# Four-layer graph network on one core: attention outputs kept in SBUF in place of the selections they used, selections rebuilt for the last pass, one copy moved from ScalarE to VectorE

## What is computed

```python
h = jnp.maximum(_layernorm(x, axis=-1), 0.0)
x = x + _L0_gnn_ref(h, ...)   # graph convolution with self loops, PReLU
x = x + _L1_gnn_ref(h, ...)   # segment_sum(edge_weight * h[src], dst) @ W.T + b
x = x + _L2_gnn_ref(h, ...)   # attention with 4 heads over edges and self loops,
                              # then batch norm over all 50,000 nodes, relu(out + h)
x = x + _L3_gnn_ref(h, ...)   # edge network on (h[src], h[dst]), segment_sum, node network
```

## Time and profile before

| | us |
|---|---|
| median of 3 runs | 2927.1 |
| lowest, highest of the runs | 2925.19, 2933.04 |
| the profiled execution's own time | 2935.71 |
| its span, first to last instruction | 2934.2 |

### The profile page before, as it was taken

The page is one execution under the profiler, slowest core; times in us unless marked ns, Lnnn a source line. Parts: engine busy times, 40 slices in busy tenths (PEclk is TensorE's granted clock), DMA queues, the critical chain, the costliest instruction groups (busy, mean ns, idle before and its releaser), DMA issues. The chain is left out here.

```text
span 2934.2 us, 52033 instructions
## 1 busy us (share of the span) xinstructions
PE 2190.3 (75%) x11215; PEld 1489.9 (51%) x11215; DVE 1814.1 (62%) x8347; ACT 1823.1 (62%) x4630; POOL 1440.1 (49%) x1442
## 2 busy tenths in 40 slices
PE   3376666666664777758885899666663999999996
PEld 1154444444443666648885444333332566666663
DVE  8787676766764666648886555466664544445552
ACT  0097777777774888859994333599995344444442
POOL 5177777777774666537771000000001366666663
PEclk9888888888886999988997999798997999999998
DMA  1155555555453555546662665499998111222210
GB/s 41 35 177 159 171 159 162 168 155 175 153 160 96 150 160 158 155 133 181 198 199 61 179 169 163 132 320 311 315 311 245 46 49 55 57 59 59 60 53 24
DMA packets 488297, 426.56 MB, mean 145 GB/s; under 512 B 54823, under 2 KB 384702, under 8 KB 488138
## 3 DMA queue, kind: packets, MB, share of 16 engines
q1 hardware_dynamic: 423946, 350.44, 39.7%
q0 software_dynamic: 64192, 74.09, 9.9%
HBM read 234.05 MB, written 194.13 MB: 146 GB/s over the span
## 5 line engine op out<-in xcount | busy, mean ns | idle before, releaser
L1982 POOL DMA_INDIRECT x_bx<-t_X,k_bslot x2 | 2.0, 1016 | 670.4 <-DMA t_X<-x_ve 670.1
L2235 POOL DMA_INDIRECT out_dram<-mlp_ou,mlp_iro x200 | 200.0, 1000 | 186.4 <-issue 185.8
L461 POOL DMA_INDIRECT second_xs<-t_X,second_irs x200 | 212.5, 1063 | 133.4 <-ACT second_m L1151 56.4
L461 POOL DMA_INDIRECT first_rd<-t_R,a_irs x200 | 203.4, 1017 | 119.0 <-issue 60.3
L2228 POOL DMA_INDIRECT mlp_xs<-t_X,mlp_irs x200 | 202.2, 1011 | 78.3 <-issue 59.7
L461 POOL DMA_INDIRECT a_xd<-in_x_dram,a_ird x200 | 207.9, 1040 | 65.7 <-issue 60.3
L461 POOL DMA_INDIRECT a_xs<-in_x_dram,a_irs x200 | 203.7, 1018 | 60.8 <-issue 60.5
L461 POOL DMA_INDIRECT project_xs<-t_X,project_irs x200 | 200.7, 1004 | 65.7 <-issue 62.2
L2278 DVE TENSOR_TENSOR mlp_v<-mlp_ps_r,mlp_b 126x512 f32<-126x512 f32 x50 | 34.6, 692 | 278.9 <-ACT mlp_y L2336 275.6
L2379 PE MATMUL mlp_ps_e<-mlp_h,mlp_we 128*128 128x504 f32 x400 | 188.4, 595 | 1.2 <-ACT mlp_h L2358 1.2
L2139 PE MATMUL x_ps_o<-x_ht,x_wd 128*128 128x512 f32 (+1 forms) x198 | 128.9, 738 | 80.7 <-ACT x_ht L2090 80.7
(11 more groups left out here) (391 smaller groups left out, 7036.4 us busy)
## 6 DMA issues: line engine op xcount, KB each, us to landing
t_X<-first_x SPq DMA_DIRECT2D x194, 256.0 KB, 3.1
first_x<-in_x_dram SPq DMA_DIRECT2D x97, 256.0 KB
project_x<-t_X SPq DMA_DIRECT2D x97, 256.0 KB, 3.1
x_x<-t_X SPq DMA_DIRECT2D x97, 256.0 KB, 6.3
t_X<-x_x SPq DMA_DIRECT2D x97, 256.0 KB, 6.0
out_dram<-x_ou SPq DMA_DIRECT2D x97, 256.0 KB, 6.7
t_G<-second_g SPq DMA_DIRECT2D x50, 267.8 KB
t_X<-first_xo SPq DMA_DIRECT2D x50, 252.0 KB
```

The lines of the kernel that those rows point to most:

```text
L461: pool.indirect_dma_start(dst[:, q, :], None, table, bass.IndirectOffsetOnAxis(ap=idx[:, q:q + 1], axis=0)).then_inc(s_rows, 16)
L2235: pool.indirect_dma_start(out, bass.IndirectOffsetOnAxis(ap=iro[s][:, q:q + 1], axis=0), OU[s][:, q, :], None, bounds_check=N - 1, oob_is_ ...
```

## The change

Three edits.

1. `kp.S0` becomes `[RW, NGE, GT * 128]`: 2048 bytes per group and partition, of which the four selections of a group take the first 2016. `kp.select(g, q)` is tile q's selection, `kp.rows(g)` the whole piece seen as four rows of 128. Attend writes its outputs to `kp.rows(g)`, where the group's selections stood; the squares go to `OQ`; `norms` becomes two products of 128 columns into two PSUM banks. The store to `T["O2"]` and its load are gone, and x3 finishes the slot rows in `kp.rows` and stores from there.
2. Since the selections are overwritten, mlp loads the rows of targets again (`dr`, 50 broadcast loads) and makes the selections again, four comparisons for each group, one group ahead. PE waits for `s_sel` beside `s_z`.
3. In second, the copy of `psA` to `AT` goes from the end of ACT's `body` to the end of DVE's.

```diff
@@ Keep
-        self.S0 = sb("S0", [RW, NT, RW])
+        self.S0 = sb("S0", [RW, NGE, GT * 128])
+    def select(self, g, q):
+        o = slice(q * RW, (q + 1) * RW)
+        if known(g):
+            return self.S0[:, g, o]
+        return self.S0[:, bass.ds(g, 1), o].rearrange("p a e -> p (a e)")
+    def rows(self, g):
+        if known(g):
+            return self.S0[:, g, :].rearrange("p (q d) -> p q d", q=GT)
+        return self.S0[:, bass.ds(g, 1), :].rearrange("p a (q d) -> p (a q) d", q=GT)
@@ second, vector, end of body
+            g3, r3 = t - 3, (u - 3) % 2
+            if there(g3, NGE):
+                dve.wait_ge(s_a, g3 + 1)
+                if not before(g3, 2):
+                    dve.wait_ge(s_y, g3 - 1)
+                dve.tensor_copy(AT[r3][:, :, :], psA[r3][:, 0:W4].rearrange("p (q e) -> p q e", q=GT)).then_inc(s_at, 1)
@@ second, scalar, end of body
-            r3 = (u - 3) % 2
-            if there(g3, NGE):
-                act.wait_ge(s_a, g3 + 1)
-                if not before(g3, 2):
-                    act.wait_ge(s_y, g3 - 1)
-                act.activation(AT[r3][:, :, :], psA[r3][:, 0:W4].rearrange("p (q e) -> p q e", q=GT), ACT.Copy).then_inc(s_at, 1)
@@ attend
-            g, s = t - 2, (u - 2) % 4
-            if there(g, NGE):
-                gate(kp, sp, s_o, g + 1)
-                sp.dma_start(slot_rows(T["O2"], g), OS[s][:, :, 0, :]).then_inc(s_os[s], 16)
...
-                if not before(g, 4):
-                    dve.wait_ge(s_os[s], landed(g - 4, s, 4))
-                    dve.wait_ge(s_n, g - 3)
...
-                    ins = dve.tensor_tensor(OS[s][:, 2 * b:2 * b + 2, 0, :].rearrange("p q (h c) -> p q h c", h=H),
+                    ins = dve.tensor_tensor(kp.rows(g)[:, 2 * b:2 * b + 2, :].rearrange("p q (h c) -> p q h c", h=H),
...
-                act.activation(OS[s][:, :, 1, :], OS[s][:, :, 0, :], ACT.Square).then_inc(s_sq, 1)
+                if not before(g, 4):
+                    act.wait_ge(s_n, g - 3)
+                act.activation(OQ[s][:, :, :], kp.rows(g), ACT.Square).then_inc(s_sq, 1)
...
-                ins = pe.matmul(psN[0:1, 0:256], kp.lastc[:, k:k + 1], OS[s][:, q, :, :].rearrange("p w d -> p (w d)"),
-                                start=k == 0, stop=k == NT - 1)
+                pe.matmul(psN[0:1, 0:128], kp.lastc[:, k:k + 1], kp.rows(g)[:, q, :], start=k == 0, stop=k == NT - 1)
+                ins = pe.matmul(psN[0:1, 512:640], kp.lastc[:, k:k + 1], OQ[s][:, q, :], start=k == 0, stop=k == NT - 1)
@@ x3
-                if not before(t, 4):
-                    gate(kp, sp, e_s3[u], landed(t - 4, u, 4))
-                sp.dma_start(Ve[u][:, :, :], erow2("O2", t)).then_inc(e_o[u], 16)
...
-                sp.dma_start(erows("X3", ge), Ve[se][:, :, :]).then_inc(e_s3[se], 16)
+                sp.dma_start(erows("X3", ge), kp.rows(ge)).then_inc(e_s3[se], 16)
...
-                dve.wait_ge(e_o[u], landed(t, u, 4))
-                dve.tensor_tensor(Ve[u][:, :, :], Ve[u][:, :, :], Sb[0:RW, :, :], ALU.mult).then_inc(e_v0, 1)
+                dve.tensor_tensor(kp.rows(t), kp.rows(t), Sb[0:RW, :, :], ALU.mult).then_inc(e_v0, 1)
@@ mlp, sync
+                r = u % 2
+                if not before(t, 2):
+                    sp.wait_ge(s_sel, t - 1)
+                sp.dma_start(dr[r][:, :].rearrange("p (k j) -> p k j", k=GT),
+                             T["dr"][bass.ds(t * GT, GT), :].partition_broadcast(RW)).then_inc(s_dr[r], 16)
@@ mlp, vector; called as select(0, 0) before the loop and select(t + 1, ...) at the end of body(t)
+        def select(t, v):
+            if there(t, NGE):
+                r = v % 2
+                dve.wait_ge(s_dr[r], landed(t, r, 2))
+                for q in range(GT):
+                    k = bass.ds(t * GT + q, 1)
+                    ins = dve.tensor_scalar(kp.select(t, q), dr[r][:, q * RW:(q + 1) * RW], kp.dcol[:, k], None, ALU.is_equal)
+                ins.then_inc(s_sel, 1)
@@ mlp, tensor
                 pe.wait_ge(s_z, t + 1)
+                pe.wait_ge(s_sel, t + 1)
```

More of the change, by code:

```diff
@@ L971, in sums @@
             gate(kp, pe, e_ci, t * GT + q + 1)
-            k = bass.ds(t * GT + q, 1)
-            s0 = kp.S0[:, k, :].rearrange("p a e -> p (a e)")
+            s0 = kp.select(t, q)
             pe.matmul(psC[0:RW, 128 * q:128 * (q + 1)], s0, M[r][:, q, :], start=True, stop=True).then_inc(e_co, 1)
@@ L1225, in sums @@
             pe.wait_ge(s_ci, g * GT + q + 1)
-            s0 = kp.S0[:, g * GT + q, :]
+            s0 = kp.select(g, q)
             pe.matmul(psC[0:RW, 128 * q:128 * (q + 1)], s0, M[s][:, q, :], start=True, stop=True).then_inc(s_co, 1)
@@ L1538, in body @@
                     k = g5 * GT + q
-                    ins = pe.matmul(psS[0:RW, q * SW:(q + 1) * SW], kp.S0[:, k, :], SAm[:, k, :], start=True, stop=True)
+                    ins = pe.matmul(psS[0:RW, q * SW:(q + 1) * SW], kp.select(g5, q), SAm[:, k, :], start=True, stop=True)
                 ins.then_inc(e_sc, 1)
@@ L1703, in phase_attend @@
     rec = sb("rec", [RW, GT, H])
-    OS = [sb(f"o{i}", [RW, GT, 2, 128]) for i in range(4)]
+    OQ = [sb(f"oq{i}", [RW, GT, 128]) for i in range(4)]
     row = sb("row", [1, 256])
     psO = [m.ps(f"o{i}", [128, 1024]) for i in range(2)]
-    psN = m.ps("norm", [128, 512])
+    psN = m.ps("norm", [128, 1024])
     psC = m.ps("norm_columns", [128, 512])
@@ L1739, in body @@
             load(t + 3, (u + 3) % 4)
-            g, s = t - 2, (u - 2) % 4
-            if there(g, NGE):
-                gate(kp, sp, s_o, g + 1)
-                sp.dma_start(slot_rows(T["O2"], g), OS[s][:, :, 0, :]).then_inc(s_os[s], 16)
         steps(sp, NGE, 3, 3, body)
-        for s in range(4):
-            sp.wait_ge(s_os[s], 16 * len(range(s, NGE, 4)))
     def heads(t, q):
@@ L1788, in _ @@
         dve.wait_ge(s_n, NGE)
-        dve.tensor_copy(row[:, :], psN[0:1, 0:256]).then_inc(s_nr, 1)
+        dve.tensor_copy(row[:, :].rearrange("p (w d) -> p w d", w=2), psN[0:1, :].rearrange("p (w d) -> p w d", w=2)[:, :, 0:128]).then_inc(s_nr, 1)
         dve.wait_ge(s_nc, 1)
@@ L1847, in body @@
                     o = column(q)
[L1848 removed]
+                    pe.matmul(psO[r][0:RW, o:o + MW], kp.select(g, q),
                               M[r][:, q, :], start=False, stop=True, skip_group_check=True).then_inc(s_co, 1)
@@ L1876, in phase_x3 @@
     Xe = [sb(f"xe{i}", [RW, GT, 128]) for i in range(4)]
-    Ve = [sb(f"ve{i}", [RW, GT, 128]) for i in range(4)]
     Ze = [sb(f"ze{i}", [RW, GT, 128]) for i in range(2)]
@@ L1890, in phase_x3 @@
     s_s3, s_so = m.ring("x3_stored", 4), m.ring("out_stored", 4)
-    e_x, e_o = m.ring("e_x2_loaded", 4), m.ring("e_o_loaded", 4)
+    e_x = m.ring("e_x2_loaded", 4)
     s_nb = sem("row_bias")
@@ L2053, in body @@
                 dve.wait_ge(e_v0, t + 1)
-                dve.tensor_tensor(Ve[u][:, :, :], Ve[u][:, :, :], Tb[0:RW, :, :], ALU.add).then_inc(e_v1, 1)
+                dve.tensor_tensor(kp.rows(t), kp.rows(t), Tb[0:RW, :, :], ALU.add).then_inc(e_v1, 1)
             for h in range(2):
@@ L2060, in body @@
                 dve.wait_ge(e_z, g + 1)
-                dve.tensor_tensor(Ve[s][:, :, :], Ve[s][:, :, :], Ze[s % 2][:, :, :], ALU.add).then_inc(e_v2, 1)
+                dve.tensor_tensor(kp.rows(g), kp.rows(g), Ze[s % 2][:, :, :], ALU.add).then_inc(e_v2, 1)
                 dve.wait_ge(e_v2, g + 1)
-                dve.scalar_tensor_tensor(Ve[s][:, :, :], Ve[s][:, :, :], 0.0, Xe[s][:, :, :], ALU.max, ALU.add).then_inc(e_x3, 1)
+                dve.scalar_tensor_tensor(kp.rows(g), kp.rows(g), 0.0, Xe[s][:, :, :], ALU.max, ALU.add).then_inc(e_x3, 1)
         steps(dve, NGE, 3, 2, body)
@@ L2172, in phase_mlp @@
     Z = [sb(f"z{i}", [RW, 2 * GT, 128]) for i in range(2)]
+    dr = [sb(f"dr{i}", [RW, W4]) for i in range(2)]
     rt = [sb(f"rt{i}", [RW, GT]) for i in range(2)]
@@ L2192, in phase_mlp @@
     s_w, s_idx, s_rows, s_xd = sem("weights"), sem("idx_ready"), kp.s_gathered, m.ring("state_loaded", 8)
+    s_dr, s_sel = m.ring("drow_loaded", 2), sem("select")
     s_st, s_mv, s_sd, s_rs, s_rt, s_z = (sem("stats"), sem("meanvar"), sem("std"), sem("rstd"), sem("rstd_last"), sem("norm"))
@@ L2269, in _ @@
         stats(0, 0)
+        select(0, 0)
         def body(t, v):
@@ L2299, in body @@
             stats(t + 1, (v + 1) % 8)
+            select(t + 1, (v + 1) % 8)
         steps(dve, NGE, 5, 3, body, 8)
@@ L2427, in body @@
                     pe.transpose(psH[0][:, q * RW:(q + 1) * RW], Z[r][:, q, :], kp.ident[0:RW, 0:RW])
-                    ins = pe.matmul(psH[1][:, q * RW:(q + 1) * RW], Z[r][:, GT + q, :], kp.S0[:, t * GT + q, :], start=True, stop=True)
+                    ins = pe.matmul(psH[1][:, q * RW:(q + 1) * RW], Z[r][:, GT + q, :], kp.select(t, q), start=True, stop=True)
                 ins.then_inc(s_t, 1)
@@ L2444, in gnn_kernel @@
         ("R", (N, 2)), ("X1", (ROWS, D)), ("X2", (ROWS, D)), ("G", (SLOTS, GW)), ("X3", (ROWS, D)),
```

(2 more changed lines are left out.)

6 lines of the change are left out of this document (1 added, 5 removed).

## The result

The changed kernel took 2886.38 us (median of 4 runs, 2878.68 to 2887.68); the kernel before, run beside it, 2929.18 us (2925.19 to 2933.04). The ratio is 0.985, 95% interval [0.983, 0.987]: 42.8 us less. The forecast was 2888, or 39 less. The profiled execution of the changed kernel took 2887.68 us, its span 2886.2.

A forecast was written before the change was run, and what follows sets the result against it. It took second as bound by a loop through engines, attend as going tile by tile, x3 by DMA, mlp by TensorE. Terms -22 - 18 + 0 + 1 = -39 us from 2927.1 gave 2888 us, range 2872 to 2912.

The forecast's parts named there:

- Second, -18: second: VectorE making the AT copy shortens the group from 6.59 to 6.2 us, gaining 18 us, ends 10 and 22.
- Rival B: second: VectorE becomes the bound, group 6.72 us, second loses 6 us; whole kernel 2912 us; chance 0.05.
- x3, -22: x3: dropping the `Ve` load of 252 KB a group gains 22 us, ends 12 and 31; ScalarE is late next.
- I take 6.95, between the ends: x3: group time chosen between 6.78 us (ScalarE without waits) and 7.16 (all TensorE waits stay), down from 7.42.
- will be late now and then: x3: DMA, at 6.6 of 6.95 us a group, is still nearly full and so sometimes late.
- cost nothing since DMA was behind anyway: x3: ScalarE's waits for TensorE, 0.38 us a group, added no time before the change because DMA held the phase.
- The calculation by 315 GB/s: x3: bytes over DMA rate set the group: 2.35 MB gives 7.45 us, 2.09 MB without the load 6.6.
- Attend, 0: attend: splitting each `norms` product into two of 128 columns costs 0; upper end 32 us if all loads are exposed.
- rival C: attend: one-column weight loads are exposed, +32 us, tile step 1.1 us; whole kernel 2920 us; chance 0.05.
- mlp, +1: mlp: four comparisons a group hide in VectorE's 5.44 us idle time; cost 1 us, ends 0 and 43.
- rival D: mlp: comparisons hold GpSimd's queue, stretching gathers or scatters, +92 us; whole kernel 2980 us; chance 0.03.
- Rival A: x3 falls only to 7.16 us a group with all ScalarE waits, second gains 10; whole kernel 2906 us; chance 0.14.

## Why the prediction was right, and where it was off

*Second, -18.* Measured -18.2 in the profiles, -18.3 alone. The group went to (1235.5 - 933.3) / 49 = 6.17 us over the whole phase, 6.2 forecast. The wait named as next (`second_hr` behind `second_bi`) is the new row, and TensorE's idle time is at the 1.1 us forecast. Rival B is out. `HT2`, moved and not removed, gave 9 us more in second: what stands inside the loops counts, and not only ScalarE's load.

*x3, -22.* The direction and the next limit were right, with ScalarE full at 6.81 us. The term was mis-sized: -29.7. The step that failed is "I take 6.95, between the ends". Its reason that DMA "will be late now and then" was wrong: ScalarE waited for node rows not once. It kept 0.17 of the 0.38 us a group that ScalarE waits for TensorE, and up to 2190 they fell to 5.2 us, or 0.11 a group. And ScalarE's group without a wait is 6.71 us, not 6.78. Behind it stands a step that was wrong in kind: these waits "cost nothing since DMA was behind anyway". They were part of the 7.42 us. The whole load put back brought the waits for node rows and for TensorE back together with the low clock, and half of the load brought next to none of them (2.1 us in 200). The calculation by 315 GB/s pointed the right way for the wrong reason: the half load ran at 327.

*Attend, 0.* It took 3.4 us more in the profiles, of which the split explains 1.5. The one-column loads are not exposed (0.95 us a tile), and rival C is out.

*mlp, +1.* Nothing that could be read, on the chips of the forecast: 613.3 us against 613.5, and from x3's last row to mlp's first product 45.5 against 43.9, which was 45.2 in the run of the copy alone, where mlp is that of before. The idle time of 5.44 was forecast to become 4.6 and is 4.75. The row against rival D was thinner than the prediction has it: the gather of 1.06 us stood beside normalizations, but the scatter of 1.02 at 2608.70 beside the statistics. The run with 20 comparisons is what settles it. That mlp with the new selections takes 100 us more on the other chips was nowhere in the prediction.

*Sum.* -39 forecast, -42.8 measured, inside the range. That it came so near is partly luck: x3 gave 7.7 us more than forecast and attend took 3.4 back. Rival A (2906) is out: it held x3 at 7.16.
